# Order of an analysis stage in a wavelet attention and FFN kernel: second level of one chunk ahead of the transposes, and two buffers for the high band

## The chip, the cores and the metric

The kernel runs on one core of one Trainium2 chip. The metric is device time in microseconds; 1209.41 us is the median of three runs of the kernel before. The engines are TensorE (PE: matmuls and transposes), VectorE (DVE), ScalarE (ACT), GpSimd (POOL) and SyncE (SP, which issues most transfers). Each runs its own list of instructions in order; they meet at semaphores only.

## The reference

Two stages follow each other, each with a residual and a layer norm.

```python
# mixer, x is (2, 4096, 512)
for _ in range(2):                       # two levels of analysis
    l = dwconv(low, h_filter)[:, ::2]    # 4 taps a channel, every second sample
    h = dwconv(low, g_filter)[:, ::2]
    highs.append(h); low = l
low = linear_attention(low, 16)          # q = k = elu(h) + 1; kv and z are sums over all positions
for h, L in zip(reversed(highs), reversed(lens)):   # two levels of synthesis
    low = dwconv(repeat(low, 2), h_synth) + dwconv(repeat(h, 2), g_synth)
x = layer_norm(x + layer_norm(x + low) * gamma + beta)
# FFN, int32 weights scaled by 1/127, hidden size 1536
x = layer_norm(x + (silu(x @ wg.T) * (x @ wu.T)) @ wd.T)
```

## The kernel before

The sequence is cut into slices of 1024 positions, four to a batch (`PER_BATCH`), and the 512 channels into four chunks of 128 partitions. The FFN runs slice by slice on TensorE, from eight iterations of `body`; analysis, attention and norms of later slices lie beside it. Attention needs sums over a whole batch, so the four slices of batch 0, and slice 4 (the first of batch 1), are analysed before the first iteration. This is **the opening**, `NPRO` = 5 slices, and the change lies in it.

In a slice a of the opening chunks 0 and 1 are filtered by ScalarE (first tap: `pro_l1`, `pro_band_firsts`) and VectorE (the other taps: `pro_low1_taps`, `pro_band_taps`). Chunks 2 and 3 are filtered by TensorE with matmuls against diagonal matrices (`conv1` for level 1, `conv2` for level 2), and ScalarE copies the results out of PSUM (`pro_out1_copy`, `pro_out2_copy`). A level-1 result is `l1` or `l1_odd`, a level-2 low band `l2` or `l2_odd`, by the parity of a; the level-2 high band is `h2_in` for slice 0, else `h2`, and SyncE stores it to `h2_scratch` (`pro_h2_store`, semaphore `st_h2`).

A slice behind, the keys are made: `pro_keys` on ScalarE, `pro_keys_sum` on VectorE, then `pro_turn` on TensorE (16 transposes to PSUM), `pro_turn_copy` on ScalarE, `pro_kv` on TensorE (64 small matmuls) and `pro_kv_add` on VectorE. SyncE stores the keys (`pro_q_store`). `pro_diags` on ScalarE makes 28 more diagonal matrices of 128 x 128 from the identity, 10 a slice in slices 1 to 3; the close of the opening uses them.

In slice 4 the denominators follow (`pro_heads`, `pro_dens`, and `dens` on VectorE with a reciprocal); SyncE's `dens` spreads them over partitions in four transfers into `att` (semaphores `ld_att`). GpSimd waits for the last of them (chunk 1) and then issues the twelve weight pieces (`load_weights`, a transfer with a cast from int32 to float16 into `w16`, 1536 columns each) and, behind them in its list, the small steps of the first norms (`CLOSE_POOL`). The tables `CLOSE_PE`, `CLOSE_ACT` and `CLOSE_DVE` give the order of the close: attention products, synthesis of slice 0, norms, and the first gate matmuls.

ScalarE writes a buffer again only when its store has landed:

```python
if a > 1:
    act.wait_ge(turned, NC * (a - 1))
    act.wait_ge(st_h2, 16 * a)
    act.wait_ge(pro_halo, 1)
```

`hold` is such a wait followed by a no-operation, so that a transfer is issued behind it. Input loads of slice a+1 (`load_pro`) are issued in slice a, each when its buffer has been read: chunk 3 behind `conv1(a, 3)`, chunks 0 and 1 behind the level-1 taps, chunk 2 behind `conv1(a, 2)`.

## Time and profile before

| | us |
|---|---|
| median of 3 runs (lowest to highest) | 1209.41 (1209.27 to 1209.95) |
| profiled execution, its own time | 1209.61 |
| profiled execution, its span | 1207.8 |
| TensorE busy | 1173.7 |
| VectorE busy | 973.1 |
| ScalarE busy | 672.6 |
| GpSimd busy | 303.1 |
| first gate matmul starts at | 120.81 |

The span is what the profile covers of the execution; the rest of its own time lies around it. TensorE's busy time includes the idle-looking latency of its last matmul in a row, so two of its rows can overlap by some tenths of a microsecond: a group's length is read from the start of one row to the start of the next. The clock that was granted to TensorE is 1.00 at 2.4 GHz and 0.50 at 1.2 GHz. In a row of the timeline the first number is the start, the second the time from there to the end of the last instruction in it, and the brackets at its end give the idle time before it and what ended that.

### The profile page before, as it was taken

The numbers are of one execution on the slowest core, as the hardware profiler recorded it, in microseconds if no ns is written. First come the engines' busy times: TensorE is split into PE (matmuls) and PEld (weight loads), VectorE is DVE, ScalarE is ACT, GpSimd is POOL, SyncE is SP. The second block draws the span as 40 slices with busy tenths as digits, with TensorE's granted clock in tenths as the row PEclk, the third lists the DMA queues.
The fourth block names the chain that finished last, engine by engine and source line by source line (L and its number), as shares of the span: only waits on it lengthen the run. The fifth ranks groups of instructions, "written<-read, shape, count | busy, mean of one in ns | idle before, by whom it ended". The sixth has DMA issues, their size and how long they took to land.

```text
span 1207.8 us, 19489 instructions
## 1 busy us (share of the span) xinstructions
PE 1173.7 (97%) x6456; PEld 604.4 (50%) x6456; DVE 973.1 (81%) x1951; ACT 672.6 (56%) x1403; POOL 303.1 (25%) x730
## 2 busy tenths in 40 slices
PE   6888999999999999999999999999999999999997
PEld 5567644445445544445445444444445444454443
DVE  7797999998999989997997779867997689845331
ACT  6954744677346854576346644666346644565342
POOL 0014322152314313152213412142304313131101
PEclk9998999999999999999999999999999999999999
DMA  7886520222212310222102310211111310110000
GB/s 263 271 201 142 184 61 19 106 97 89 71 44 79 128 40 18 98 83 74 36 27 97 98 35 18 105 62 53 35 58 64 106 35 11 42 55 1 3 34 35
DMA packets 52301, 92.96 MB, mean 77 GB/s; under 512 B 9072, under 2 KB 28784, under 8 KB 51312
## 3 DMA queue, kind: packets, MB, share of 16 engines
q1 hardware_dynamic: 50480, 87.10, 21.9%
q0 software_dynamic: 1728, 4.72, 2.2%
q8 instruction: 46, 0.75, 0.3%
q14 instruction: 47, 0.39, 0.1%
HBM read 67.09 MB, written 25.19 MB: 76 GB/s over the span
## 4 chain that ended last, share of the span: by engine, by line
PE 81%; DVE 6%; ACT 5%; issue 4%; POOL 3%; DMA 1%; SPq 0%; POOLq 0%; ACTq 0%; DVEq 0%
PE ps_up L679 12%; PE ps_up L680 12%; PE ps_gate L679 12%; PE ps_gate L680 12%; PE ps_down L698 12%; PE ps_down L697 12%; PE ps_x L622 2%; PE ps_y L640 2%; DVE l L1286 1%; PE ps_x L601 1%; POOL rs L1216 1%; PE ps_down L864 1%; DVE h L1286 1%; ACT x_hi L1136 1%; DVE hid L1286 1%
## 5 line engine op out<-in xcount | busy, mean ns | idle before, releaser
L697 PE MATMUL ps_down<-w,hid 128*128 128x512 f16 x768 | 291.4, 379 | 1.2 <-DVE hid L1672 1.0
L698 PE MATMUL ps_down<-w,hid 128*128 128x512 f16 x768 | 291.3, 379 | 0.0
L679 PE MATMUL ps_up<-x_hi,w 128*128 128x512 f16 x760 | 288.4, 379 | 0.9 <-DVE h_f L1685 0.9
L679 PE MATMUL ps_gate<-x_hi,w 128*128 128x512 f16 x760 | 288.4, 379 | 0.5 <-ACT h_f L1160 0.5
L680 PE MATMUL ps_gate<-x_lo,w 128*128 128x512 f16 x760 | 288.3, 379 | 0.0
L680 PE MATMUL ps_up<-x_lo,w 128*128 128x512 f16 x760 | 288.2, 379 | 0.0
L1160 ACT ACTIVATE h_f<-ps_gate 128x512 f32<-128x512 f32 x192 | 113.9, 593 | 205.6 <-PE ps_gate L680 204.6
L1685 DVE SCALAR_TENSOR_TENSOR h_f<-ps_up,h_f 128x512 f32<-128x512 f32 x192 | 130.9, 685 | 110.1 <-PE ps_up L680 97.7
L1152 ACT ACTIVATE hid<-h_f 128x512 f16<-128x512 f32 x192 | 119.7, 623 | 42.0 <-DVE h_f L1685 42.0
L1672 DVE TENSOR_TENSOR hid<-h_f,hid 128x512 f16<-128x512 f32 x192 | 130.9, 682 | 1.9 <-ACT hid L1152 1.0
L679 PEld LDWEIGHTS ps_up<-x_hi,w 128*128 128x128 f16 x760 | 74.2, 98 | 91.5 <-DVE h_f L1685 1.8
L680 PEld LDWEIGHTS ps_up<-x_lo,w 128*128 128x128 f16 x760 | 74.3, 98 | 89.4
L697 PEld LDWEIGHTS ps_down<-w,hid 128*128 128x128 f16 x768 | 75.0, 98 | 85.2 <-issue 1.5
L698 PEld LDWEIGHTS ps_down<-w,hid 128*128 128x128 f16 x768 | 75.1, 98 | 84.2
L679 PEld LDWEIGHTS ps_gate<-x_hi,w 128*128 128x128 f16 x760 | 74.2, 98 | 83.0 <-ACT h_f L1160 2.0
L680 PEld LDWEIGHTS ps_gate<-x_lo,w 128*128 128x128 f16 x760 | 74.3, 98 | 82.7
L1213 POOL TENSOR_SCALAR rs<-rs 128x1 f32<-128x1 f32 x128 | 46.4, 363 | 216.5 <-ACT x_hi L1136 142.6
L1286 DVE SCALAR_TENSOR_TENSOR s_chan<-low,coef,s_chan 128x512 f32<-128x512 f32 x140 | 98.8, 747 | 1.0
L1216 POOL TENSOR_TENSOR rs<-rs,minus_half 128x1 f32<-128x1 f32 x128 | 95.8, 749 | 10.7
L1699 DVE SCALAR_TENSOR_TENSOR x<-ps_down,x 128x512 f32<-128x512 f32 x64 | 44.1, 689 | 55.5 <-PE ps_down L698 54.9
L966 ACT ACTIVATE x<-x,rs 128x512 f32<-128x512 f32 x64 | 51.8, 809 | 64.3 <-POOL rs L1218 64.2
L1192 POOL TENSOR_TENSOR rs<-rs,minus_part 128x1 f32<-128x1 f32 x64 | 18.8, 294 | 212.6 <-ACT x L945 212.1
(260 smaller groups left out, 1688.0 us busy)
## 6 DMA issues: line engine op xcount, KB each, us to landing
xt<-x_tok SPq DMA_DIRECT2D x64, 256.0 KB, 2.7
out<-x SPq DMA_DIRECT2D x64, 256.0 KB, 2.0
xb<-x_chan SPq DMA_DIRECT2D x7, 2060.0 KB, 7.7
xa<-x_chan SPq DMA_DIRECT2D x20, 515.0 KB, 5.0
w<-weights POOLq DMA_DIRECT2D x12, 384.0 KB, 9.9
att<-den SPq DMA_DIRECT2D x32, 129.5 KB, 2.7
xa<-x_phase SPq DMA_DIRECT2D x8, 515.0 KB, 6.4
q_in<-q_scratch SPq DMA_DIRECT2D x7, 518.0 KB, 4.5
```

What stands on the lines that cost most here:

```text
L679: pe.matmul(ps_gu[k % 2][g][:, :], w, x1_hi[:, b, c, :], start=(c == 0), stop=False)
L680: mm = pe.matmul(ps_gu[k % 2][g][:, :], w, x1_lo[:, b, c, :], start=False, stop=(c == NC - 1))
L697: pe.matmul(ps_d[t % 2][:, :], h_hi[:, k, t * P:(t + 1) * P], w, start=(k == 0), stop=False)
L698: mm = pe.matmul(ps_d[t % 2][:, :], h_lo[:, k, t * P:(t + 1) * P], w, start=False, stop=(k == NH - 1))
L966: nc.scalar.activation(x1[:, t, :], x1[:, t, :], ACT.Identity, bias=rs2[:, t, 5:6], scale=rs2[:, t, 4:5]).then_inc(x1_ready, 1)
L1152: nc.scalar.activation(h_hi[:, k, :], h_f[:, k % RING, :], ACT.Copy).then_inc(hi_done, 1)
L1160: nc.scalar.activation(h_f[:, k % RING, :], ps_gu[k % 2][0][:, :], ACT.Silu, scale=WSCALE / X1_SCALE).then_inc(silu_done, 1)
L1213: nc.gpsimd.tensor_scalar(rs[:, 3:4], rs[:, 2:3], shrink / C, eps * shrink, ALU.mult, ALU.add).then_inc(var, 1)
L1216: nc.gpsimd.tensor_tensor(rs[:, 4:5], rs[:, 3:4], minus_half[:, :], ALU.pow).then_inc(rstd, 1)
L1286: return V.scalar_tensor_tensor(out=acc, in0=src, scalar=coef[:, c, n:n + 1], in1=acc if add is None else add, op0=ALU.mult, op1=ALU.add)
L1672: V.tensor_tensor(h_lo[:, k, :], h_f[:, k % RING, :], h_hi[:, k, :], ALU.subtract).then_inc(lo_done, 1)
L1685: V.scalar_tensor_tensor(out=h_f[:, k % RING, :], in0=ps_gu[k % 2][1][:, :], scalar=WSCALE * H_SCALE / X1_SCALE, in1=h_f[:, k % RING, :], ...
```

## The change

In five places:

- **TensorE.** `conv2(a, 3)` moves ahead of the transposes of slice a-1, directly behind the two level-1 groups. `pro_kv` comes behind `conv2(a, 2)`; in slice 4 it stays ahead of it.
- **ScalarE.** The 28 diagonals are spread by `DIAGS`: 4 before everything, 5 behind the band firsts of slice 0, 3 each behind the turn copies of slices 1, 2 and 3, and in slice 4 five ahead of the band firsts and five behind the turn copies. The first taps of slice a+1 (`pro_l1`) move ahead of the second pair of level-2 copies.
- **High band.** The odd slices use a new buffer `h2_odd`, which lies in the last two pieces' room of `w16`; its stores count on `st_h2_odd`. A write waits for the store of two slices back (`h2_free`), and GpSimd waits for both odd stores before it issues the tenth and later weight pieces (index 10).
- **SyncE.** The loads of chunks 2 and 3 of `xb` move from slices 1 and 2 to slice 4, behind the high-band store of slice 3; the four token loads follow; then the key store of slice 3 and the denominators' broadcast; the four input loads of slice 5 come behind the broadcast, and the zero pads behind them.
- **VectorE.** The four `xbeta` adds move ahead of the wait for `pro_out2`.

```diff
+DIAGS = ((0, 4), (4, 5), (9, 3), (12, 3), (15, 3), (23, 5), (18, 5))
@@
+        h2_odd = w16[:, PIECES * PW - 2 * NC * M2:PIECES * PW].bitcast(F32).rearrange("p (c n) -> p c n", c=NC)
@@
+        h2_pro = (h2_in[:, :, 1:1 + M2], h2_odd, h2[:, :, :], h2_odd, h2[:, :, :])
+
         def h2_of(a, c):
-            return h2_in[:, c, 1:1 + M2] if a == 0 else h2[:, c, :]
+            return h2_pro[a][:, c, :]
+
+        def st_h2_of(a):
+            return st_h2 if a % 2 == 0 else st_h2_odd
+
+        def h2_free(eng, a):
+            if a > 2:
+                hold(eng, st_h2_of(a), 16 if a == 3 else 32)
@@ load_bands
-                hold(sp, st_h2, 16 * PER_BATCH * (batch + 1))
+                hold(sp, st_h2_odd, 32)
+                hold(sp, st_h2, 16 * PER_BATCH * (batch + 1) - 32)
@@ SyncE, the opening
                 if a > 0:
                     pro_h2_store(a - 1)
+                    if a == PER_BATCH:
+                        for c in (2, 3):
+                            sp.dma_start(xb[:, c, :], x_chan[:, 0, c, :]).then_inc(ld_xb0, 16)
+                        for t in range(4):
+                            load_xt(0, t)
+                    if a == PER_BATCH:
+                        pro_q_store(a - 1)
+                        dens(0, 0, 0)
                     hold(sp, pro_conv1, 2 * a + 1)
                     load_pro(a + 1, 3)
                     hold(sp, pro_low1, 6 * (a + 1))
                     load_pro(a + 1, 0)
                     load_pro(a + 1, 1)
-                    pro_q_store(a - 1)
+                    if a < PER_BATCH:
+                        pro_q_store(a - 1)
                     hold(sp, pro_conv1, 2 * a + 2)
                     load_pro(a + 1, 2)
-                if a in (1, 2):
-                    sp.dma_start(xb[:, a + 1, :], x_chan[:, 0, a + 1, :]).then_inc(ld_xb0, 16)
-                if a == PER_BATCH:
-                    for t in range(4):
-                        load_xt(0, t)
-
-            dens(0, 0, 0)
@@ TensorE
                 conv1(a, 3)
                 conv1(a, 2)
+                conv2(a, 3)
                 if a > 0:
                     for c in range(NC):
                         pro_turn(a - 1, c)
                 if a == PER_BATCH:
                     pro_dens()
                     pro_kv(a - 1)
-                conv2(a, 3)
+                conv2(a, 2)
                 if 0 < a < PER_BATCH:
                     pro_kv(a - 1)
-                conv2(a, 2)
@@ ScalarE, pro_band_firsts and pro_out2_copy
-                    act.wait_ge(st_h2, 16 * a)
+                    h2_free(act, a)
@@ ScalarE, the opening
+                    pro_diags(*DIAGS[0])
...
+                if a == PER_BATCH:
+                    pro_diags(*DIAGS[a + 2])
                 pro_band_firsts(a, 0)
                 pro_band_firsts(a, 1)
+                if a == 0:
+                    act.wait_ge(coef_ready, 6)
+                    pro_diags(*DIAGS[1])
...
-                if a == 1:
-                    act.wait_ge(coef_ready, 6)
-                if 1 <= a <= 3:
-                    pro_diags(10 * (a - 1), 10)
+                if a > 0:
+                    pro_diags(*DIAGS[a + 1])
                 pro_out2_copy(a, 3)
-                pro_out2_copy(a, 2)
                 if a < PER_BATCH:
                     pro_l1(a + 1, 0)
                     pro_l1(a + 1, 1)
+                pro_out2_copy(a, 2)
                 pro_keys(a, 0)
@@ GpSimd, load_weights
+                    if n == PIECES - 2:
+                        nc.gpsimd.wait_ge(st_h2_odd, 32)
@@ VectorE, behind the last slice
+            for t in range(DSUB):
+                xbeta(0, 0, t)
             dve.wait_ge(pro_out2, 2 * NPRO)
```

TensorE's list in slice 1, from the last level-1 group to the last level-2 group, in the kernel before (`kvt_mem` holds the diagonals, `hid` holds `l1_odd` as well as the turned keys; `ps_gate1` and `ps_up1` serve level 1 and the transposes):

```order
L747 MATMUL ps_up0<-xa,kvt_mem 64x257 x4
L782 MATMUL ps_x<-ident,q_in 128x128 x2
L782 MATMUL ps_x<-ident,l2 128x128 x2
L782 MATMUL ps_y<-ident,q_in 128x128 x2
L782 MATMUL ps_y<-ident,l2 128x128 x2
L782 MATMUL ps_gate1<-ident,q_in 128x128 x2
L782 MATMUL ps_gate1<-ident,l2 128x128 x2
L782 MATMUL ps_up1<-ident,q_in 128x128 x2
L782 MATMUL ps_up1<-ident,l2 128x128 x2
L763 MATMUL ps_down0<-hid,kvt_mem 64x256 x8
L572 MATMUL ps_x<-hid 32x32 x32
L763 MATMUL ps_down1<-hid,kvt_mem 64x256 x8
```

And in the kernel after:

```order
L761 MATMUL ps_up0<-xa,kvt_mem 64x257 x4
L777 MATMUL ps_down0<-hid,kvt_mem 64x256 x8
L796 MATMUL ps_x<-ident,q_in 128x128 x2
L796 MATMUL ps_x<-ident,l2 128x128 x2
L796 MATMUL ps_y<-ident,q_in 128x128 x2
L796 MATMUL ps_y<-ident,l2 128x128 x2
L796 MATMUL ps_gate1<-ident,q_in 128x128 x2
L796 MATMUL ps_gate1<-ident,l2 128x128 x2
L796 MATMUL ps_up1<-ident,q_in 128x128 x2
L796 MATMUL ps_up1<-ident,l2 128x128 x2
L777 MATMUL ps_down1<-hid,kvt_mem 64x256 x8
L586 MATMUL ps_x<-hid 32x32 x32
```

The group of eight matmuls to `ps_down0` (level 2 of chunk 3; order counts a matmul of four passes once) has gone ahead of the transposes, and the small products behind the group to `ps_down1`.

ScalarE's list of the same slice, from the diagonals to the keys, before:

```order
L983 ACTIVATE kvt_mem<-ident,coef 128x128 x8
L983 ACTIVATE h_f<-ident,coef 128x128 x2
L980 ACTIVATE hid<-ps_down0 128x256
L980 ACTIVATE h2<-ps_down0 128x256
L980 ACTIVATE hid<-ps_down1 128x256
L980 ACTIVATE h2<-ps_down1 128x256
L983 ACTIVATE l1<-xa,coef 128x514 x2
L1045 ACTIVATE keys<-hid 128x512
L1047 ACTIVATE keys<-keys 128x512
L1045 ACTIVATE keys<-hid 128x512
L1047 ACTIVATE keys<-keys 128x512
```

After:

```order
L997 ACTIVATE h_f<-ident,coef 128x128 x3
L994 ACTIVATE hid<-ps_down0 128x256
L994 ACTIVATE w16<-ps_down0 128x256
L997 ACTIVATE l1<-xa,coef 128x514 x2
L994 ACTIVATE hid<-ps_down1 128x256
L994 ACTIVATE w16<-ps_down1 128x256
L1059 ACTIVATE keys<-hid 128x512
L1061 ACTIVATE keys<-keys 128x512
L1059 ACTIVATE keys<-hid 128x512
L1061 ACTIVATE keys<-keys 128x512
```

Three diagonals stand where ten stood, the copies to `h2` go to `w16`, and the first taps of slice 2 (`l1<-xa,coef`) stand between the two pairs of copies.

SyncE's list at the end of the opening, before:

```order
L415 DMA xa<-x_phase 128x1030
L486 DMA h2_scratch<-h2 128x4x256
L408 DMA xa<-x_chan 128x1030 x3
L491 DMA q_scratch<-keys 128x4x256
L408 DMA xa<-x_chan 128x1030
L450 DMA xt<-x_tok 128x512 x4
L470 DMA att<-den 128x1x259 x4
L528 DMA q_scratch<-zeros 1024x1x1
L528 DMA q_scratch<-zeros 1024x1x2
```

After:

```order
L426 DMA xa<-x_phase 128x1030
L497 DMA h2_scratch<-w16 128x4x256
L523 DMA xb<-x_chan 128x1030 x2
L462 DMA xt<-x_tok 128x512 x4
L502 DMA q_scratch<-keys 128x4x256
L482 DMA att<-den 128x1x259 x4
L419 DMA xa<-x_chan 128x1030 x4
L542 DMA q_scratch<-zeros 1024x1x1
L542 DMA q_scratch<-zeros 1024x1x2
```

The broadcast (`att<-den`) has two loads of `xb` and the token loads ahead of it and no load of `xa`; the four of `xa` come behind it.

## Rows read from the trace of the kernel before

**Rows 1.** The page: busy time of the fullest engine, share of the span, instructions.

```profile
PE 1173.7 (97%) x6456; PEld 604.4 (50%) x6456; DVE 973.1 (81%) x1951; ACT 672.6 (56%) x1403; POOL 303.1 (25%) x730
```

**Rows 2.** Busy times by stretch, length first; then clock, transfers' busy share, GB/s.

```profile
core 0: us, PE busy (x) PEld busy (x) DVE busy (x) ACT busy (x) POOL busy (x), PEclk, DMA share, GB/s
...
44.60:55.60 11.00, 8.71 (x121) 6.31 (x120) 10.69 (x28) 10.42 (x27) 0.00 (x0) 0.84 0.86 280
...
105.90:111.20 5.30, 5.29 (x13) 4.22 (x14) 4.46 (x11) 2.22 (x5) 4.15 (x8) 0.50 0.86 214
...
120.70:1207.80 1087.10, 1077.53 (x5559) 529.25 (x5557) 877.70 (x1691) 595.89 (x1207) 284.12 (x679) 1.00 0.18 61
```

**Rows 3.** Timeline of VectorE, slices 2 to 4 (start, length, engine, line, operation).

```profile
31.47 4.08 DVE L1286 SCALAR_TENSOR_TENSOR l<-xa,coef,l 128x514 f32<-128x514 f32 x6 [1.73 <-ACT l L983]
...
44.59 4.07 DVE L1286 SCALAR_TENSOR_TENSOR hid<-xa,coef,hid 128x513 f32<-128x513 f32 x6 [2.40 <-ACT hid L983]
...
50.20 0.48 DVE L1286 SCALAR_TENSOR_TENSOR hid<-hid,coef 128x256 f32<-128x256 f32 x1
...
55.27 0.29 DVE L1542 TENSOR_TENSOR kv_sum<-ps_x,kv_sum 128x128 f32<-128x128 f32 x1 [0.23 <-PE ps_x L572]
58.49 4.08 DVE L1286 SCALAR_TENSOR_TENSOR l<-xa,coef,l 128x513 f32<-128x513 f32 x6 [2.93 <-ACT l L983]
```

**Rows 4.** Timeline of ScalarE in slice 3: first taps, band firsts, diagonals, level-2 copies.

```profile
43.76 1.46 ACT L983 ACTIVATE hid<-xa,coef 128x513 f32<-128x513 f32 x2
...
48.65 0.53 ACT L983 ACTIVATE hid<-hid,coef 128x256 f32<-128x256 f32 x1 [0.52 <-DMA h_scratch<-h]
...
52.79 1.30 ACT L983 ACTIVATE h_f<-ident,coef 128x128 f32<-128x128 f32 x4
...
55.13 0.39 ACT L980 ACTIVATE hid<-ps_down 128x256 f32<-128x256 f32 x1
```

**Rows 5.** Timeline of TensorE: level 1 of chunk 2 (slice 2), transposes, level 2.

```profile
32.57 1.13 PE L747 MATMUL ps_gate<-xa,kvt_mem 128*64 128x257 f32 x8 [0.76 <-DMA xa<-x_phase]
...
49.06 0.44 PE L782 MATMUL ps_x<-ident,keys 128*128 128x128 f32 x2 [2.29 <-DVE keys L1526]
...
51.78 2.75 PE L763 MATMUL ps_down<-hid,kvt_mem 128*64 128x256 f32 x16
...
55.16 1.95 PE L763 MATMUL ps_down<-hid,kvt_mem 128*64 128x256 f32 x16
```

**Rows 6.** Transfers from 0 to 110 us: KB each, median us to landing.

```profile
xa<-x_phase SPq DMA_DIRECT2D x8, 515.0 KB, 6.4
...
h_scratch<-h SPq DMA_DIRECT2D x3, 512.0 KB, 4.5
```

**Rows 7.** The page, transfers of the whole kernel: the denominators' broadcast.

```profile
att<-den SPq DMA_DIRECT2D x32, 129.5 KB, 2.7
```

**Rows 8.** The chain of waits, in order of time: start, length.

```profile
71.84 5.83 DMA att<-den
```

**Rows 9.** The weight transfers: shortest, median and longest time to landing.

```profile
DMA to landing us min/median/max: 4.5/9.9/15.4
```

**Rows 10.** Timeline of GpSimd and of ScalarE's first norm step, 78 to 101 us.

```profile
78.29 3.95 POOL L1187 DMA_DIRECT2D w<-weights  x7 [36.09 <-DMA att<-den]
...
97.22 0.19 ACT L945 ACTIVATION_READ_ACCUMULATOR x<-ps_x 128x1 f32 x1
97.44 2.66 POOL L1187 DMA_DIRECT2D w<-weights  x5 [15.20 <-issue]
...
100.07 0.25 POOL L1192 TENSOR_TENSOR rs<-rs,minus_part 128x1 f32<-128x1 f32 x1
```

**Rows 11.** Busy times by stretch, as in rows 2, beside the weight transfers.

```profile
80.00:82.00 2.00, 2.00 (x20) 2.00 (x19) 2.00 (x6) 0.21 (x2) 2.00 (x5) 1.00 0.90 51
...
84.00:86.00 2.00, 2.00 (x11) 1.74 (x11) 2.00 (x7) 0.47 (x2) 0.00 (x0) 1.00 1.08 211
```

**Rows 12.** Timeline of VectorE: the first attention product.

```profile
77.17 0.43 DVE L1556 TENSOR_TENSOR att<-ps_x,att 128x259 f32<-128x259 f32 x1
```

More of the change, by code:

```diff
@@ L1660, in _ @@
                        "norm2b": lambda t: norm2_scale(0, t), "norm3": lambda t: norm3(0, 0, t)}
-            for t in range(DSUB):
-                xbeta(0, 0, t)
             for name, n in CLOSE_DVE:
```

11 lines of the change are left out of this document (5 added, 6 removed).

## Prediction

> **What bounds the kernel now.** I read the page first, for which engine is full: TensorE, 97% of the span [rows 1]. The busy times by stretch say where that holds [rows 2]. From 120.70 us on TensorE is busy for 1077.53 of 1087.10 us, so nothing that the change touches there can move the time. Before that lies the opening, in which four stages follow each other: five slices of analysis (to about 72.6 us), the close of the attention, and the first norms. Whatever makes the first gate matmul start earlier shortens the kernel by as much. The profiled execution took 1209.61 us for its span of 1207.8, 0.2 above the median of 1209.41; a shift in the span is taken off the median.
>
> The timeline of VectorE shows what the slices wait for [rows 3]. Its low-band taps of slices 2, 3 and 4 start at 31.47, 44.59 and 58.49 us, each behind an idle time of 1.73, 2.40 and 2.93 us, ended by ScalarE. So the distance between two starts is over 13 us, and VectorE's own work in it is 5.61 us (taps and key sums, 44.59 to 50.20), 4.84 us (second-level taps, to 55.27 less 0.23 idle) and 0.28 us: 10.7 us. ScalarE, which ends those waits, runs the first taps last, behind eight to ten diagonals and four copies [rows 4]. TensorE in turn idles 2.29 us before the transposes, and its clock reads 0.84 over that slice, which means some of it at 1.2 GHz [rows 2, 5].
>
> Behind the slices, the chain of waits goes: denominators, their broadcast (landing at 77.67, 5.83 us after the issue), GpSimd's weight DMAs, GpSimd's first norm at 100.07 [rows 8, 10]. GpSimd starts seven weight pieces at 78.29, stands still for 15.20 us, issues the other five for 2.66 us, and only then does the norm that ScalarE had ready at 97.41 [rows 10]. The 15.4 us of the slowest piece [rows 9] show that the eighth is issued about when the seventh (issued at 81.7) has landed. All behind it, to the first gate matmul, is in a row with that norm, so what counts is when the weight train ends.
>
> **Slices.** The first taps of slice a+1 now stand ahead of the second pair of level-2 copies, and the diagonals are spread: 4 at the start, where ScalarE waits for the input, 5 in slice 0, then 3, 3, 3 and 10 in slice 4. One diagonal is 0.29 us (eight from 52.79 to 55.13 [rows 4]). In slice 1 that takes 7 diagonals and 2 copies (0.53 us) out of the way: 2.6 us against a wait of 1.73, so VectorE starts slice 2 without one, at 29.7. The five in slice 0 delay TensorE's second-level group of chunk 2 by 1.5 us, but the keys behind it wait for VectorE's taps anyway; cost nothing, and 1.5 if that cover were gone.
>
> From there ScalarE needs per slice: first taps, keys and level-1 copy 4.37 us (43.76 to 48.65 less 0.52 idle), band firsts, copy and turns 4.14 us (48.65 to 52.79), 3 diagonals 0.88, level-2 copies 1.1: 10.5 us, below VectorE's 10.7. The 0.52 us wait for the store of the high band goes, since the store two slices back has landed (4.5 us for such a store [rows 6]; it now has over 15). TensorE is the third: four groups of 16 matmuls at 1.95 us, transposes about 1.8, products 0.7: 10.3 us [rows 5]. Level 2 of chunk 3 ahead of the transposes fills its 2.29 us of idle time. This order has a price: the transposes now come behind a group that wants the load of chunk 2. In slice 2 that load lands at 32.57 [rows 5], 1.1 us after the old start but 2.8 us after the new one. Two groups (3.7 us) and the first transposes (0.4) behind it end at 36.9, where ScalarE, 6.25 us into the slice, would be at 35.95: 0.9 us late, of which about 0.5 is left after the slack between 10.5 and 10.7. In the next slices everything, the issue of the load too, has moved with the slice, so there I take 0 to 0.3. Starts: 29.7, 40.8, 51.4, against 58.49: **7.1 us earlier**. Bounds: 8.0 (a pace of 10.4) down to 4.1 (rival 1). The clock at 1.2 GHz in slice 3 stood behind TensorE's idle stretch; with under 1 us of idle time per slice I expect full clock.
>
> Moving bytes is not far from a bound either. A slice stores 1.0 and loads 2.1 MB, 3.1 MB in 10.8 us: 287 GB/s, where the rows show 280 at a busy share of 0.86, so 326 when full [rows 2]. The two loads of chunks 2 and 3 for the close no longer lie in slices 1 and 2, which is what makes room.
>
> Writing the high band into the weights' room, and the taps on it, is not in the trace. Same partitions, same widths as the old buffer; I take zero, with plus or minus 0.1 us per slice.
>
> **Slice 4.** Five diagonals (1.5 us) ahead of the band firsts: ScalarE is ready about 55.4, the firsts run 56.9 to 58.6, VectorE could start them at 57.65 and waits 0.3. The transposes come after level 2 of chunk 3, and the denominators need turn copies 0 and 1 (60.1), so their product ends at 60.9, 0.5 us behind VectorE's chunk 0. Together 0.7 us given back: denominators ready **6.35 us earlier**. The other five diagonals lie where ScalarE waits for TensorE.
>
> **SyncE's queue and the broadcast.** Before, 4.1 MB were issued from the last high-band store to the broadcast, the last of it just ahead, and the broadcast landed 5.83 us after its issue [rows 8]. Now it is 3.1 MB (store 0.5, two loads 1.0, tokens 1.0, keys 0.5), issued from 52.6 to 57.5 and moved at 326 GB/s by about 63, when the broadcast is issued. Over the kernel such a broadcast lands in 2.7 us [rows 7]. Between 2.7 and 5.83 I take 3.0, nearest to the first since the queue is then empty: **2.8 us earlier** on top, bounds 0 and 3.1. The loads for the close land by 62.5 and are wanted at 63.6; the tokens land before their adds, which ends a 0.9 us wait of VectorE's.
>
> **The weight train.** The four loads of slice 5 (2.06 MB, 6.3 us at 326 GB/s) and the four zero-pad DMAs no longer precede the weights but run beside them. Before, the train took from 78.29 to 97.1, 18.8 us; seven pieces of 393 KB at 211 GB/s are 13.0 of it [rows 9 to 11]. Now the loads are issued from 66.4 on and the first piece at 69.2. About 3 us pass before weight bytes move, in which 4 us of the loads are done; some 1.9 us of loads and 1.2 us more of pads stay in front or beside: **3.1 us later**. Bounds: 0 and 6.3. The wait for the odd stores before the tenth piece costs nothing: behind it are two pieces and all the norms on GpSimd, but the store landed near 57. The extra hold on SyncE before each later band load has half an iteration's slack.
>
> **Sum.** 6.35 + 2.8 - 3.1 = 6.0 us for GpSimd's first norm: 94.1 instead of 100.07. The other path, VectorE's first attention product (at 77.17 [rows 12]), moves by 6.15 + 0.9 = 7.0 us, so ScalarE's 97.41 becomes 90.4: still earlier than GpSimd, and the train decides. Behind it the same row of waits follows, 1.2 GHz stretch included (clock 0.50 from 105.90 to 111.20 [rows 2]). 1209.41 - 6.0 = **1203.4 us**.
>
> A rule speaks to the last term. The trace shows 51 GB/s at a busy share of 0.90 from 80 to 82 us, when pads and weights overlap, so pads do take room [rows 11]. The Trainium skill, DMA: Bandwidth & Descriptors, Queues, rings and completion order, has each DMA engine take turns between queues packet by packet; by it the tiny pads would cost the weights next to nothing. That makes the fourth case below.
>
> **Rivals.**
> 1. *The load of chunk 2 sets the pace.* If it lands 1 us later in each slice (6.4 us is the median from issue to landing [rows 6]; it now stands before level 2, the transposes and their copies), the pace is 11.9: 3 us less, 1206.4. For it: TensorE has no slack left. Against: fewer bytes in the queue.
> 2. *The broadcast lands as late as before*, 5.8 us after the issue: 2.8 us less, 1206.2. Against: the queue runs empty by my count.
> 3. *The change does not do what it says*: another wait takes the whole of each stall (keys waiting for their store, say), and only the exchange in the queue is left, 2.8 - 3.1: 1209.7.
> 4. *The train is no longer than before* (18.8 us), because loads and pads use only the time in which its first piece is being prepared: GpSimd is free 6.35 + 2.8 = 9.1 us earlier, and VectorE's path decides with 7.0: 1202.4.
> 5. *Slower: TensorE at 1.2 GHz through the slices.* A group of 16 took 2.75 instead of 1.95 us in slice 3 [rows 5]: 4 x 2.75 + 2.7 + 0.7 = 14.4 us per slice against 13.1 now, 3 x 1.3 = 3.9 us later, and 0.3 for the queue: 1213.6. It decides from a pace of 13.0 on. Against: TensorE idles less than before.
>
> **How the numbers follow.** Forecast 0.52, rival 1 0.17, rival 2 0.08, rival 3 0.06, rival 4 0.12, rival 5 0.05. The range, 1201.0 to 1208.0, reaches from rival 4 with 1.4 us for the 1.2 GHz stretch in the norms to rivals 1 and 2 with their spread; outside lie 3, 5 and tails, about 0.2. A measurement of this kernel tells 0.2% (2.4 us) from no change. Faster: the first two, fourth and forecast, less the tail of rivals 1 and 2, 0.83; within 0.2%: 0.11; slower: 0.06.
>
> **What would show it.** Right: no idle time of VectorE over 0.5 us before the taps of slices 2 to 4, which start near 29.7, 40.8 and 51.4; clock 1.00 in them; broadcast landing near 68.5, first weight piece near 69.2, GpSimd's first norm near 94, first gate matmul near 114.7. Wrong if the load of chunk 2 keeps TensorE waiting over 2 us per slice, or if GpSimd's pause exceeds 19 us.

## The result and the profile after

The changed kernel ran in 1201.28 us (median of 4 runs, 1199.3 to 1201.86) beside 1209.68 for the kernel before: a ratio of 0.9926, interval 0.9912 to 0.9940. That is 8.4 us faster where 6.0 were forecast. Taken off the 1209.41 of the forecast by its ratio it is 1200.5, a little below the range on record (1201.0 to 1208.0); 1201.28 as it stands lies just inside it. In two later series, each on a chip of its own, it had 1205.17 us (6 runs, 1202.72 to 1207.17; ratio 0.9972, 0.9960 to 0.9984) and 1202.73 (5 runs, 1201.39 to 1204.34; 0.9951, 0.9938 to 0.9965). All 15 runs together have a median of 1202.73, about 6 below before. That this is the forecast of 6.0 is luck, as its terms will show. So two things need a cause: where the terms of the forecast went in the profiled execution, and why one kernel spreads over 8 us.

The profiled execution took 1201.81 us, its span 1200.0, against 1207.8. The page, to be held against [rows 1]:

```profile
PE 1170.5 (98%) x6456; PEld 601.5 (50%) x6456; DVE 972.8 (81%) x1951; ACT 673.0 (56%) x1403; POOL 303.4 (25%) x730
```

The busy times by stretch (columns as in [rows 2]): two stretches of slice 0, the last group of the close (at 0.50 from 105.90 before), and all from the first gate matmul on.

```profile
16.00:18.00 2.00, 1.37 (x10) 0.84 (x12) 2.00 (x6) 2.00 (x7) 0.00 (x0) 0.77 0.56 196
18.00:20.00 2.00, 2.00 (x12) 1.21 (x10) 2.00 (x5) 0.48 (x2) 0.00 (x0) 0.50 0.00 0
100.90:105.30 4.40, 4.40 (x21) 3.82 (x22) 3.82 (x10) 2.22 (x5) 3.25 (x8) 1.00 1.08 237
113.00:1200.00 1087.00, 1077.47 (x5558) 529.76 (x5556) 877.20 (x1691) 595.98 (x1207) 284.44 (x679) 1.00 0.19 61
```

From the first gate matmul (113.06 us, before 120.81) to the end it is the same 1087 us: all of the gain lies ahead of it. VectorE's low-band taps, the answer to [rows 3], start slices 2, 3 and 4 at 30.41, 42.27 and 54.39; the rest of each group waits once more, for ScalarE, whose own wait there was for the load of a chunk:

```profile
30.41 0.76 DVE L1306 SCALAR_TENSOR_TENSOR l<-xa,coef,l 128x514 f32<-128x514 f32 x1
31.44 3.41 DVE L1306 SCALAR_TENSOR_TENSOR l<-xa,coef,l 128x514 f32<-128x514 f32 x5 [0.27 <-ACT l L997]
42.27 0.75 DVE L1306 SCALAR_TENSOR_TENSOR hid<-xa,coef,hid 128x513 f32<-128x513 f32 x1 [0.37 <-ACT hid L997]
43.56 3.40 DVE L1306 SCALAR_TENSOR_TENSOR hid<-xa,coef,hid 128x513 f32<-128x513 f32 x5 [0.54 <-ACT hid L997]
54.39 4.07 DVE L1306 SCALAR_TENSOR_TENSOR l<-xa,coef,l 128x513 f32<-128x513 f32 x6
```

TensorE, to be read against [rows 5]: in slice 0 it now waits 2.15 us for the copy behind the five diagonals, and the group of 16 behind that gap takes 3.28 us; in slices 2 to 4 it waits for the load of chunk 2.

```profile
16.63 3.28 PE L777 MATMUL ps_down<-l,kvt_mem 128*64 128x256 f32 x16 [2.15 <-ACT l L994]
33.31 1.13 PE L761 MATMUL ps_gate<-xa,kvt_mem 128*64 128x257 f32 x8 [1.25 <-DMA xa<-x_phase]
45.61 0.22 PE L757 MATMUL ps_gate<-zeros,kvt_mem 128*64 128x1 f32 x1 [1.84 <-DMA xa<-x_phase]
56.58 0.22 PE L754 MATMUL ps_gate<-zeros,kvt_mem 128*64 128x1 f32 x1 [0.32 <-DMA xa<-x_phase]
```

Behind the slices, the broadcast from SyncE's queue (second fence: the landing of its last transfer by the chain of waits, 3.04 us, where [rows 8] has 5.83), then GpSimd's weights and first norm, against 78.29, 15.20 and 100.07 in [rows 10]:

```profile
66.49 3.26 SPq L482 DMA_DIRECT2D att<-den  x4
```

```profile
69.15 3.04 DMA att<-den
```

```profile
72.81 3.95 POOL L1207 DMA_DIRECT2D w<-weights  x7 [31.36 <-DMA att<-den]
92.44 2.66 POOL L1207 DMA_DIRECT2D w<-weights  x5 [15.68 <-issue]
95.06 0.25 POOL L1212 TENSOR_TENSOR rs<-rs,minus_part 128x1 f32<-128x1 f32 x1
```

The rest of the 7.75 us is in TensorE's last group of the close, 20 matmuls. Before, it ran from 105.91 to 113.05, 7.1 us, most of it at half clock; now it takes 4.4. First twelve matmuls before, then after:

```profile
105.91 2.90 PE L864 MATMUL ps_down<-h,h_f 128*128 128x256 f32 x6 [3.12 <-ACT hid L980]
108.59 2.77 PE L864 MATMUL ps_down<-hid,h_f 128*128 128x256 f32 x6
```

```profile
100.90 1.53 PE L878 MATMUL ps_down<-h,h_f 128*128 128x256 f32 x6 [3.01 <-ACT hid L994]
102.27 1.46 PE L878 MATMUL ps_down<-hid,h_f 128*128 128x256 f32 x6
```

So 5.0 us come with GpSimd's norm, and 2.7 from a clock that did not fall. From that norm to the start of the group it is 5.84 us in both.

### The profile page after: what moved, and what is told of

It is laid out like the page before. It is cut to its first block, busy times and chain, and to the rows that moved or that the text cites. A ratio compares the mean times of both kernels' runs of the same rounds, so it can differ in the third digit from the quotient of the medians.

```text
span 1200.0 us, 19493 instructions
## 1 busy us (share of the span) xinstructions
PE 1170.5 (98%) x6456; PEld 601.5 (50%) x6456; DVE 972.8 (81%) x1951; ACT 673.0 (56%) x1403; POOL 303.4 (25%) x730
## 4 chain that ended last, share of the span: by engine, by line
PE 81%; DVE 6%; ACT 4%; issue 4%; POOL 3%; DMA 2%; SPq 0%; POOLq 0%; DVEq 0%; ACTq 0%
PE ps_up L693 13%; PE ps_up L694 13%; PE ps_gate L693 12%; PE ps_gate L694 12%; PE ps_down L711 12%; PE ps_down L712 12%; PE ps_x L636 2%; PE ps_y L654 2%; DVE l L1306 2%; PE ps_x L615 1%; POOL rs L1236 1%; DVE h L1306 1%; PE ps_down L878 1%; DMA xa<-x_phase 1%; ACT x_hi L1154 1%
## 5 line engine op out<-in xcount | busy, mean ns | idle before, releaser
L1236 POOL TENSOR_TENSOR rs<-rs,minus_half 128x1 f32<-128x1 f32 x128 | 95.9, 749 | 10.7
## 6 DMA issues: line engine op xcount, KB each, us to landing
w<-weights POOLq DMA_DIRECT2D x12, 384.0 KB, 11.1
```

Of the source, the lines that this page charges most:

```text
L1236: nc.gpsimd.tensor_tensor(rs[:, 4:5], rs[:, 3:4], minus_half[:, :], ALU.pow).then_inc(rstd, 1)
```

## The experiments

Four questions: what the clock does ahead of that group, what each half of the change brings, what the five diagonals of slice 0 cost, and what holds the pace of the slices. A last part tries a version that beats both kernels. Each series had the kernel before on the same chip, with medians 1208.94 (e1 to e4), 1209.10 (e5 to e8), 1208.69 (e9 to e12), 1208.74 (e13 to e16).

**The clock ahead of the last group.** The filler covers TensorE's gap there with work that nobody reads.

```diff
+            def fill(n):
+                pe.wait_ge(pro_low_ready, 8)
+                for _ in range(n):
+                    pe.matmul(ps_d[0][:, 0:P], ident[:, :], ident[:, :], start=True, stop=True)
...
-("norm1", 2), ("s", (2, 1)), ("norm1", 3),
+("norm1", 2), ("fill", 11), ("s", (2, 1)), ("norm1", 3),
```

> The kernel before, with 11 small matmuls (identity by identity, into a bank that is overwritten next) put into TensorE's idle time of 3.1 us ahead of the synthesis group at 105.91 us. Theory: the 2.8 us that the changed kernel gains behind GpSimd's first norm are TensorE's clock, which stayed at 2.4 GHz in it and read 0.50 from 105.9 to 111.2 us in the kernel before. Then this kernel keeps 1.00 there, its synthesis group of 20 matmuls takes 4.4 us instead of 7.3, and it is 2.5 to 3.0 us faster. Rival: the gain comes from the new order of loads and adds (earlier tokens, no pads in the way); then filling the gap is worth 0, within 0.3 us.

The kernel before with the filler: 1206.90 us (11 runs), ratio 0.9984 (0.9975 to 0.9993). In the trace the group, from 105.39 on, takes 1.53, 1.46, 1.03 and 1.03 us for its pieces, 4.4 in all instead of 7.1, and the first gate matmul comes at 117.54, 3.3 earlier, of which 0.55 is an earlier start of the weights (77.74). The trace gives the 2.7 us that the theory wanted (2.5 to 3.0); the medians give 2.0, less than it wanted, and far from the rival's 0.3.

> The changed kernel with eleven extra matmuls (identity by identity, into a bank that nobody reads any more) between the third transposes of the first norm and the last group of the close, in the only long gap of TensorE ahead of that group. Theory (2.8 us of the result come from the clock, which no longer falls ahead of this group): the changed kernel already has the full clock there in most executions, so the filler brings next to nothing: 0 to 0.7 us faster, first gate matmul between 112.5 and 113.1 us. Rival (the matmuls fill, as such, changes something else that saves 2 us, as a shorter wait behind the group): it would save about 2 us here too, first gate matmul near 111.

Measured: 1202.43 us, ratio 0.9949 (0.9936 to 0.9961), first gate matmul at 112.91, as the theory had it (112.5 to 113.1), so the rival's 111 is out. It is 0.15 earlier than in the profile of after, which had the clock whole there. Against that profile the filler gives nothing, so it is worth only what the clock takes. (This series had no changed kernel without it on the same chip.)

> The changed kernel as it is, so that the runs beside it have it on the same chip. Its first four runs gave a median of 1201.28 us. Theory (time before the first gate matmul is given away whenever TensorE's clock falls, and where it falls differs from execution to execution): the runs spread over 3 us or more, with the mean granted clock of the slower ones below that of the faster, median 1201 to 1203.5. Rival (the kernel has one time): the spread stays under 1.5 us.

The changed kernel, unchanged: 1205.17 us, ratio 0.9972, above the 1201 to 1203.5 that was expected, with the spread that was expected (4.5 us). Of its six runs the fastest, 1202.72, has a mean granted clock of 0.998, and the two at 0.997 took 1204.11 and 1206.05 and the three at 0.995 took 1204.87 to 1207.17. The profile is of the fastest. Even in it the same group fell to the lower clock, and its first twelve matmuls, behind a gap of 2.39 us, took 4.35 us where the profile of after has 2.66 (100.90 to 103.56):

```profile
99.99 2.10 PE L878 MATMUL ps_down<-h,h_f 128*128 128x256 f32 x6 [2.39 <-ACT hid L994]
101.88 2.62 PE L878 MATMUL ps_down<-hid,h_f 128*128 128x256 f32 x6
```

> The changed kernel once more, beside e14 to e16 on the same chip. Theory (it has two kinds of execution, with the clock whole and with the clock down ahead of the last group of the close): runs between 1199.5 and 1207, the lower ones at a mean clock of 0.998 or more, median 1201 to 1205. Rival (the difference between 1201.28 and 1205.17 is the chip's, not the execution's): all runs within 1.5 us of each other.

> The changed kernel with the eleven matmuls in the gap ahead of the last group of the close, as e5. Theory: the median is 1 to 3 us below that of e13, the range at its upper end smaller, last group 4.4 us in the trace. Rival (the filler is worth nothing, the kernel has simply a spread): median and spread as e13's, within 0.7 us.

On one chip: 1202.73 us for the changed kernel (1201.39 to 1204.34), 1201.02 with the filler (1200.43 to 1201.81), ratios 0.9951 and 0.9939. The medians are 1.7 us apart, the spread is 2.95 against 1.4 us. The intervals of the ratios (0.9938 to 0.9965 and 0.9926 to 0.9953) overlap, so five runs of each make the filler's gain likely; the trace is what shows it, with a group of 4.4 us (e14) against 6.1 (e13). In e13's trace the gap ahead of the group is 3.01 us, to the digit that of the first profile, and this time the clock fell. The timeline, and the stretch by its busy times, with a granted clock of 0.61 (third number from the right):

```profile
99.00 2.03 PE L878 MATMUL ps_down<-h,h_f 128*128 128x256 f32 x6 [3.01 <-ACT hid L994]
100.83 2.69 PE L878 MATMUL ps_down<-hid,h_f 128*128 128x256 f32 x6
```

```profile
99.00:103.40 4.40, 4.40 (x13) 3.54 (x14) 3.83 (x10) 2.23 (x5) 3.25 (x8) 0.61 1.08 237
```

Over all profiled executions without a filler (before, after, e2, e3, e4, e8, e9, e13) the gap is 2.0 to 3.1 us and the clock fell in seven of eight; the exception is the profile of after. In the ten with a filler it is 0.7 us at most and the clock fell in none. The length of the gap alone does not decide, though. In e8 TensorE stood 3.70 us in slice 2, longer than anywhere above, and the clock stayed whole behind it (1.00, third number from the right in the stretch):

```profile
35.36 1.13 PE L761 MATMUL ps_gate<-xa,kvt_mem 128*64 128x257 f32 x8 [3.70 <-DMA xa<-x_phase]
```

```profile
36.00:38.00 2.00, 2.00 (x20) 1.23 (x17) 1.97 (x8) 1.03 (x4) 0.42 (x2) 1.00 1.06 268
```

The kernel before has both in one execution: 2.31 us ahead of the transposes of slice 1, clock whole, and 2.29 us ahead of those of slice 3 [rows 5], clock down.

The rival, that the difference between 1201.28 and 1205.17 is the chip's, is not excluded. Its mark, all runs of e13 within 1.5 us of each other, is missed (2.95). Nor is the theory of two kinds of execution shown: e13's profiled one, with the clock down in the last group, took 1201.94 us, and the first profile, with the clock whole there, 1201.81, since e13's slice 4 started 3 us earlier.

**The two halves of the change.**

Kernel e2 is the one before with SyncE's loop as changed, e3 the changed one with SyncE's loop as before:

```diff
+                    if a == PER_BATCH:
+                        for c in (2, 3):
+                            sp.dma_start(xb[:, c, :], x_chan[:, 0, c, :]).then_inc(ld_xb0, 16)
+                        for t in range(4):
+                            load_xt(0, t)
+                    if a == PER_BATCH:
+                        pro_q_store(a - 1)
+                        dens(0, 0, 0)
```

> The kernel before with SyncE's new order alone (loads for the close in slice 4, broadcast ahead of the loads of slice 5). Theory: the slices start as before (58.5 us for the last), since ScalarE sets their pace there; the broadcast lands 2.4 us sooner after its issue and the weight train is 0.5 us longer, so GpSimd's first norm moves by 1.5 to 2.5 us, and with the smaller gap the clock may stay up: 2 to 5 us faster. Rival (the prediction's price for the train, 3.1 us): about 0, within 0.5 us.

> The kernel after with SyncE's old order: the two loads for the close back in slices 1 and 2, the loads of slice 5 ahead of the broadcast. Theory that the queue of loads sets the slices' pace: two more loads of 0.5 MB in slices 1 and 2 make the starts of slices 3 and 4 0.5 to 2 us later than 42.3 and 54.4, the broadcast lands 2.4 us later, and the kernel is 3 to 6 us slower than the kernel after. Rival that ScalarE's and TensorE's order sets the pace: same starts, 2 us slower.

e2: 1205.93 us, ratio 0.9972 (0.9963 to 0.9982). The slices start as before (31.16, 44.14, 58.03), the weights at 74.59 instead of 78.29, the first norm at 97.13, the first gate matmul at 116.81. e3: 1205.93 us, 0.9977 (0.9967 to 0.9987): slice 4 at 55.53, weights at 75.36, first norm at 97.33, first gate matmul at 117.01. In e2 the slices did not move and the first norm came 2.9 us earlier, more than the 1.5 to 2.5 of the theory; the rival, no change, is out. In e3 slice 3 did not come later than in the profile of after (41.86 against 42.27), slice 4 came 1.1 us later, and the time is 3 to 6 us above the changed kernel's 1201.28 as expected, but on another chip.

Alone the queue brings 4.0 us at the first gate matmul and the rest of the change 3.8; together, 7.75. That the sum fits is luck. At GpSimd's first norm the two bring 2.9 and 2.7, 5.7 in all, where the profile of after has 5.0; behind it they bring 1.06 each, since the clock fell only in part of the last group, where after has 2.7. The clock fell in other places in each of the three (in slice 0 it held in e3 and fell in after), so whether the halves add up is not shown. Each alone is worth about half.

**The diagonals of slice 0.**

```diff
-                if a == 0:
-                    act.wait_ge(coef_ready, 6)
-                    pro_diags(*DIAGS[1])
                 pro_out1_copy(a, 2)
 ...
                 pro_out2_copy(a, 2)
+                if a == 0:
+                    act.wait_ge(coef_ready, 6)
+                    pro_diags(*DIAGS[1])
                 pro_keys(a, 0)
```

> The kernel after with the five diagonals of slice 0 behind the last level-2 copy instead of ahead of the level-1 copy of chunk 2. Theory: there they let TensorE idle 2.15 us, the clock fell to 1.2 GHz, the first store was issued at 20.7 instead of 19.3 us and the next load of chunk 3 at 22.2 instead of 19.8, and all loads behind them in the queue were late. Without that: clock 1.00 from 16 to 22 us, slice 2 starts by 29.8 instead of 30.4 and slice 4 by 53.5 instead of 54.4, kernel 0.8 to 2 us faster. Rival (the prediction: cover hides it): 0, within 0.3 us.

> The changed kernel with the five slice-0 diagonals behind the level-2 copies, as e4, and the filler as well. In e4 the first norm came 1.8 us earlier and the group behind it gave 1.7 us back at a clock of 1.2 GHz. Theory: with the filler the group takes 4.4 us instead of about 6, first gate matmul near 111.3, 1.5 to 1.9 us faster than the changed kernel. Rival (the gain of e4 was lost to something later in the chain than the clock, as the other path through VectorE): first gate matmul stays near 112.9.

> As e14, and eight more matmuls, identity by identity, between the two second-level groups of slice 0, where TensorE waits 2.15 us for the diagonals. Theory (the five diagonals cost their delay of 1.5 us, and behind it the clock: the group behind the gap took 3.28 instead of 1.95 us at a granted clock of 0.50): the group takes 1.95 us, the store of slice 0's high band and the loads behind it are issued 1.0 to 1.3 us earlier, slice 4 starts 0.4 to 1.3 us earlier than 54.39. Rival (the clock falls there whatever TensorE does, or the loads do not hang on it): group over 2.7 us, or slice 4 within 0.3 us of 54.4.

e4: 1202.65 us, ratio 0.9947 (0.9934 to 0.9960), not the 0.8 to 2 us below 1201.28 that was expected. Slice 4 starts at 52.47, 1.9 us earlier than in the profile of after, the first norm comes at 93.25, 1.8 earlier, and the first gate matmul at 112.92, 0.14 earlier: the last group fell to the lower clock and took the gain. With the filler (e6) the group takes its 4.4 us and the first gate matmul comes at 111.47, 1.6 us earlier than in after; the median, 1201.81 us (ratio 0.9945), doesn't show it, in a spread of 1200.16 to 1205.03.

e15 leaves the diagonals where they are and covers only the gap that they make: 1201.41 us, 0.9937 (0.9924 to 0.9951), slice 4 at 52.20, first gate matmul at 110.95, the earliest of all kernels that give the reference's output. Its slice 0 and that of e13, where nothing covers the gap:

```profile
15.09 2.05 PE L896 MATMUL ps_x<-ident 128*128 128x128 f32 x16
17.07 1.95 PE L777 MATMUL ps_down<-l,kvt_mem 128*64 128x256 f32 x16
```

```profile
16.68 1.95 PE L777 MATMUL ps_down<-l,kvt_mem 128*64 128x256 f32 x16 [1.82 <-ACT l L994]
```

The other profiles help here. Up to slice 4 their lists are those of after, but for the filler in slice 0 of e15 and the place of the diagonals in the row of e4. The gap in slice 0, the group of 16 behind it, and the starts of slices 2, 3 and 4:

| | gap | group | slice 2 | slice 3 | slice 4 |
|---|---|---|---|---|---|
| after | 2.15 | 3.28 | 30.41 | 42.27 | 54.39 |
| e5 | 2.15 | 3.62 | 30.89 | 42.22 | 54.03 |
| e11 | 2.05 | 2.76 | 30.98 | 42.33 | 54.48 |
| e9 | 1.39 | 1.95 | 29.37 | 41.03 | 53.06 |
| e14 | 1.25 | 1.95 | 29.21 | 40.90 | 52.94 |
| e13 | 1.82 | 1.95 | 29.28 | 40.21 | 51.43 |
| e15 (gap filled) | none | 1.95 | 29.52 | 41.06 | 52.20 |
| e4, e6, e12, e16 (diagonals later) | 0.42 to 0.64 | 1.95 | 29.30 to 29.64 | 40.66 to 40.95 | 52.47 to 53.18 |
| forecast | | | 29.7 | 40.8 | 51.4 |

So the diagonals' delay by itself costs nothing that shows: with the clock whole, slice 2 starts at 29.2 to 29.5 with them in place and at 29.3 to 29.6 without. Where the clock fell behind the gap it starts 0.9 to 1.8 us later than with the diagonals and the clock whole, and slice 4 is still 0.8 us or more later. In the profile of after, with 3.28 us for the group, the store of slice 0's high band is issued at 20.69 instead of 19.41 (e13), the load behind it at 22.17 instead of 20.55. The 1.5 us that e15's text gives the delay was wrong; moving the diagonals helps because the gap shrinks (0.60 us in e6). e15 went the way of its theory, but not by its sizes: the store came at 19.80, 0.9 us earlier instead of 1.0 to 1.3, and slice 4 2.2 us earlier instead of 0.4 to 1.3. The slices behind slice 2 spread by more than the clock explains: from slice 2 to slice 4 the seven rows need 22.2 to 24.0 us.

**The pace of the slices.**

e7, SyncE's order:

```diff
                     load_pro(a + 1, 1)
-                    if a < PER_BATCH:
-                        pro_q_store(a - 1)
                     hold(sp, pro_conv1, 2 * a + 2)
                     load_pro(a + 1, 2)
+                    if a < PER_BATCH:
+                        pro_q_store(a - 1)
```

> The changed kernel with the filler and with the store of the keys (0.5 MB) behind the load of chunk 2 in SyncE's queue instead of ahead of it, in slices 1 to 3. Theory (TensorE's waits of 1.25, 1.84 and 0.32 us for that load in slices 2 to 4 hold the pace): they shrink by up to 1.6 us (0.5 MB at 326 GB/s), slice 4 starts 1 to 2.5 us earlier than the 54.39 of the changed kernel, and the first gate matmul 1 to 2 us earlier. Rival (the pace is held by the loads of chunks 0 and 1, for which ScalarE waits, or by the late start in slice 0): slice 4 starts within 0.5 us of 54.4, no change of the time.

The theory falls: TensorE no longer waits for chunk 2 in any slice, yet slices 2 and 3 start at 30.99 and 41.88 (its second chunk 43.09), where e5, with the filler alone and the same half clock in slice 0, has 30.89 and 42.22 (43.15). The wait has only moved, to ScalarE's keys, which want the late store landed; behind it TensorE stood 2.54 us, and its clock fell (3.57 us for the group), so slice 4 starts at 56.84. Time 1202.99 us, ratio 0.9945.

```profile
45.40 0.63 ACT L1065 ACTIVATE keys<-l 128x512 f32<-128x512 f32 x1 [1.81 <-DMA q_scratch<-keys]
48.47 3.57 PE L777 MATMUL ps_down<-hid,kvt_mem 128*64 128x256 f32 x16 [2.54 <-ACT hid L1000]
```

e8, TensorE's order:

```diff
                 conv1(a, 2)
-                conv2(a, 3)
                 if a > 0:
                     for c in range(NC):
                         pro_turn(a - 1, c)
...
+                conv2(a, 3)
                 conv2(a, 2)
```

> The changed kernel with TensorE's order of before: level 2 of chunk 3 behind the transposes, all else as changed. Theory (this reorder is what takes TensorE's 2.3 us of idle time away, the price being the wait for chunk 2's load): slice 4 starts 1.0 to 3.0 us later than 54.39, the time is 1 to 3 us longer than the changed kernel's. Rival (with the wait for the load the reorder gains nothing net, the gain is ScalarE's): slice 4 within 0.5 us of 54.4, same time.

With TensorE's old order slices 3 and 4 start at 43.87 and 55.10 (second chunk 56.36). Against the 54.39 of after that is 0.7 us later, between the theory (1.0 to 3.0) and the rival (0.5). But here the clock of slice 0 held, and against the profiles in which it held too (e9, e13, e14) the second chunk is 2.1 to 3.7 us later. In this profile one wait for chunk 2 is 3.70 us, so the wait that I feared from the new order is there without it. The time, 1202.98 us over a spread of 8 (1200.99 to 1209.26; ratio 0.9956), decides nothing; one trace speaks for the reorder.

e10, with the keys' store cut alike:

```diff
-                sp.dma_start(h2_dram[:, 0, :, a * M2 + 1:(a + 1) * M2 + 1], h2_pro[a])
+                sp.dma_start(h2_dram[:, 0, :, a * M2 + 1:a * M2 + 65], h2_pro[a][:, :, 0:64])
```

> The kernel of e6 with the stores of keys and high band in slices 0 to 3 cut from 256 columns to 64, so 0.26 MB a slice instead of 1.05; what is left out is written behind the opening with other values, so the output of the first block is not the reference's. Theory (the 3.1 MB that a slice moves hold its pace near 11.7 us, through whichever load is wanted first): with 2.35 MB the waits for loads go and slices 2, 3 and 4 start 10.6 to 10.9 us apart, slice 4 near 51.2 instead of 53.18. Rival (the loads are late because they are issued late in the slice, and their time from issue to landing does not come from the bytes beside them): landings stay 5.5 to 7.5 us, slice 4 within 0.5 us of 53.2.

Slices 2, 3 and 4 start at 29.30, 40.44 and 51.65, 11.14 and 11.21 us apart, where e6 has 11.34 and 12.23. First the two stretches of e10, then those of e6; the second column is the length, the fourth VectorE's busy time:

```profile
29.30:40.44 11.14, 10.29 (x148) 6.61 (x146) 10.80 (x30) 10.59 (x25) 0.76 (x4) 1.00 0.76 225
40.44:51.65 11.21, 10.87 (x156) 7.71 (x153) 10.79 (x29) 10.55 (x26) 0.00 (x0) 1.00 0.75 215
```

```profile
29.61:40.95 11.34, 10.58 (x152) 7.24 (x150) 10.69 (x29) 10.33 (x25) 0.86 (x4) 1.00 0.84 264
40.95:53.18 12.23, 10.13 (x150) 7.53 (x148) 10.93 (x29) 10.92 (x26) 0.00 (x0) 1.00 0.89 289
```

VectorE's own work is 10.8 us, as the prediction had it (10.7); what stands above it is waiting, 0.3 and 0.4 us a slice with small stores, 0.65 and 1.3 with the full ones. Three more profiles have e6's lists up to slice 4 (e4, e12, e16): with e6 they need 11.06 to 11.39 us from slice 2 to slice 3, where e10 has 11.14, and 11.78 to 12.27 from there to slice 4, where e10 has 11.21. So a quarter fewer bytes buy nothing in the first stretch and 0.6 to 1.1 us in the second; slice 4 is 0.8 to 1.5 us earlier, at 51.65. The rival's 53.2 within 0.5 is out, and the theory's 10.6 to 10.9 us a slice is not reached. How the bytes do it is only half seen: the loads' time from issue to landing hardly changes (channel loads 5.8 us, 5.6 in e6; phase loads 5.9 and 6.2), as the rival said, while the stores of the keys land in 6.0 instead of 7.4 us, and ScalarE's waits for them, 0.55 and 0.35 us in e6, are gone. The first gate matmul comes at 109.49, 2.0 us earlier than in e6. The time, 1200.83 us, shows less of it: from there to the end this kernel takes 1088.4 us instead of 1087, perhaps for the columns that it writes behind the opening.

**GpSimd's norms, and a version beyond both.**

```diff
-            load_weights(0, PIECES)
+            load_weights(0, 7)
+            behind = {("norm1", 1): 7, ("norm2", 1): 8, ("norm2", 2): 9, ("norm1q", 3): 10, ("norm2", 3): 11}
             for name, t in CLOSE_POOL:
                 steps[name](0, 0, t)
+                if (name, t) in behind:
+                    load_weights(behind[name, t], 1)
```

> The changed kernel with the filler, and with GpSimd's last five weight pieces put one by one between its norm instructions instead of ahead of them all. Theory (GpSimd stands still until the seventh piece has landed, so the row of norms waits for the weight train, and without that it would wait only for ScalarE, which has x ready at 93.27 us against 95.06 in GpSimd): first norm at 93.3, first gate matmul 1.0 to 1.8 us earlier (111.3 to 112.1), time 1.0 to 1.8 us shorter than the changed kernel's. Rival (the issues between the norms, 0.53 us each, or the late pieces give it back): first gate matmul at 112.9 or later.

> Three of these together on the changed kernel: slice-0 diagonals later (e6), filler (e5), norms between the weight pieces (e11). Theory: 1.6 us from the diagonals and 1.0 to 1.8 from the norms add up, since the path through VectorE and ScalarE moves with the slices: first gate matmul at 109.7 to 110.5, 1198.5 to 1200 us. Rival (the path through VectorE's attention products does not move with the diagonals, as it is held by the broadcast): no more than either alone, first gate matmul near 111.4.

> The kernel of e12 (diagonals of slice 0 later, filler, norms between the weight pieces) again, on another chip beside the changed kernel. Theory: 2.5 to 4.5 us below e13 and 1.0 to 2.5 below e14, ratio to the kernel before 0.992 to 0.9935. Rival (its 1200.04 us was luck of the executions): within 1 us of e14.

In e11 GpSimd's first norm starts at 93.44, when ScalarE has x ready, but takes 0.97 us instead of 0.25; the next starts at 95.42, against 96.09 in e5, and the first gate matmul at 112.34, 0.6 earlier: less than the 1.0 expected, since half of the gain went into that slow first instruction. Time 1201.65 us, 0.9940 (0.9927 to 0.9954), on the chip where the changed kernel had 1205.17. e12, with the diagonals later: first gate matmul at 111.03, later than the 109.7 to 110.5 of its theory, 1200.04 us, 0.9935 (0.9922 to 0.9949). Against e5 (112.91) the diagonals alone bring 1.4 us there (e6), the norms alone 0.6 and both 1.9, so they nearly add; the theory had both terms too large. e16, the same on another chip: 1200.69 us, 0.9935, beside 1202.73 for the changed kernel and 1201.02 with the filler alone. Its theory, 2.5 to 4.5 us below e13 and 1.0 to 2.5 below e14, fails (2.0 and 0.3), and the rival, within 1 us of e14, holds. Its median is below both kernels', but e14 and e15 are as fast within the noise: most of it is the filler's.

## Why the prediction was wrong

By its own steps, for the profiled executions:

- **What bounds the kernel.** Right: the row of waits, the place of the gain, and that GpSimd's norm decides and not the path through VectorE (x ready at 93.27, norm at 95.06).
- **Slices, 7.1 us earlier.** 4.1 in the profile. Two steps failed. One is that the five diagonals in slice 0 "cost nothing, and 1.5 if that cover were gone". The cover held; what was put at nothing is TensorE's own gap of 2.15 us, in a place where it had had none (granted clock 1.00 from 14 to 20 us before), and the half clock behind it, 0.9 to 1.8 us at slice 2. The other is the pace behind slice 2, next point. e13 has the starts of the forecast (29.28, 40.21 and 51.43 against 29.7, 40.8 and 51.4), but it is the best of the profiles: with the clock as whole, e9 and e14 reach slice 4 at 53.06 and 52.94.
- **"In the next slices [...] I take 0 to 0.3".** The clock was full in slices 2 to 4, as forecast, but TensorE's waits for chunk 2 were 1.25, 1.84 and 0.32 us, where the forecast had a delay of 0.9 us in slice 2 (0.7 by its own terms: 32.57 + 3.7 + 0.4 is 36.7) and 0 to 0.3 behind it. The slices lie 11.86 and 12.12 us apart, where the forecast had 11.1 and 10.6 and rival 1 had 11.9. Its 3 us less is what the slices lost here, though in part for the clock of slice 0 and so by luck. Rival 1 had the load right; e10 shows that the bytes beside it have a part, and e7 that without this wait another one (the keys' for their store) takes its place.
- **Slice 4, 0.7 us given back.** 1.1: VectorE waits 0.79 us for the denominators' product (64.18, before 67.21).
- **Broadcast, 2.8 us earlier.** 2.4. The landing took 3.04 us, the 3.0 of the forecast; the four issues took 0.4 us longer than before.
- **Weight train, 3.1 us longer.** 0.5, from 19.15 to 19.63 (19.15, not 18.8, is what [rows 10] gives: 78.29 to 97.44). This step, "some 1.9 us of loads and 1.2 us more of pads stay in front or beside", failed by 2.6 us. In the first stretch of the train, in which weights hardly moved before (51 GB/s in [rows 11]), 389 GB/s passed (rows below), so most of what the loads needed was free, and the weights kept their rate beside the pads. Rival 4 named this mechanism with 0.12. The other profiles with the new queue give 0.3 to 1.4 us, so not quite free. The wait for the odd stores (ahead of index 10, the eleventh piece) cost nothing, as forecast: the last five issues take 2.66 us in both.
- **"The same row of waits follows, 1.2 GHz stretch included".** The row of waits did (5.84 us from norm to group in both), the stretch did not in the profile of after: 2.7 us, of which the range had allowed 1.4. Without it the profile would stand at 1209.41 - 5.0 = 1204.4 us, well inside the range; with it at 1201.7, near its end, and the 0.6 us from there to the medians' 8.4 is spread of the executions. In e4, e9 and e13 the clock did fall, for part of the group. The forecast took a thing that falls one way or the other for a fixed cost.

The weight train by stretches, around the issue of its first seven pieces (72.81 to 76.76 us) and while pads and weights run side by side (last two numbers: share of the DMA engines, GB/s):

```profile
72.00:76.00 4.00, 2.67 (x15) 1.76 (x14) 3.94 (x17) 3.72 (x11) 3.19 (x6) 1.00 0.99 389
78.00:82.00 4.00, 4.00 (x28) 3.74 (x27) 4.00 (x12) 0.56 (x3) 0.00 (x0) 1.00 1.17 212
82.00:86.00 4.00, 4.00 (x20) 3.48 (x20) 3.91 (x13) 0.00 (x0) 0.00 (x0) 1.00 1.16 210
```

SyncE's queue is held by the last two pad DMAs for 15.51 us from 76.28 on, and the weights beside it move at 210 to 212 GB/s, the 211 of [rows 11] without pads. The turn-taking between queues, packet by packet, of the Trainium skill (DMA: Bandwidth & Descriptors, Queues, rings and completion order) fits this; a kernel without the pads was not tried.

In sum 3.03 + 2.45 - 0.48 = 5.0 us at GpSimd's norm instead of 6.0: 3.3 us less from the slices and 2.6 more from the train nearly cancel, which is luck. With 2.7 us of clock on top it is 7.75 of span. In e13 it is 6.9 at the norm (93.17) and 1.1 in the group. The spread between whole runs is explained for the profiled ones only: in all of them but e10 the time from the first gate matmul to the end is 1086.9 to 1087.3 us, so nearly all they differ in lies ahead of it. For the others there is the mean clock. 0.995 instead of 0.998 over 1204 us is, by my estimate, 3.6 us of lost work, which is about what separates e9's median from the first one. But it does not account for all: one run of e7 took 1203.62 us at 1.000 and one of e6, with the filler, 1204.73 at 0.998. Where the clock fell in the runs without a trace is open, what else slows them too, and so is what makes the same gap of 3.01 us end in one clock or the other.

## What to carry to other kernels

A term that ends in a gap of the bounding engine has two prices, the gap and the clock behind it, and the second may fall in one execution and not in the next: look at the clock of a stretch in more than one profile, give the range both, and cover the gap with work that nobody reads before comparing anything finer. It does not end every spread: e6 and e12 have the filler and spread over 4.9 and 4.2 us. When a transfer is moved in front of another one, ask first when the second one's bytes begin to move; here 2 MB passed ahead of them for 0.3 to 1.4 us. And when two terms of a forecast miss by 3 us each, a total that fits proves neither.

## What the runs showed of the hardware

- Ahead of the last group of the close the clock fell behind gaps of TensorE of 2.0 to 3.1 us in seven of eight executions, and never behind 0.7 us or less in ten. In slice 0 it fell behind gaps of 2.05 and 2.15 us in four (after, e5, e7, e11), while behind 2.15 (e8), 1.82, 1.40, 1.39 and 1.25 us it held. It held also behind 3.70 us in slice 2 of e8 and behind 2.22 us in slice 4 of e15, so more than the length of the gap decides.
- GpSimd's stand ahead of its eighth piece of weights was 15.2 to 15.4 us in the three profiled executions with the old queue (before, e1, e3) and 15.45 to 16.6 us in the twelve with the new one that issue the pieces in one row; in e11, e12 and e16 the eighth piece, issued after 95 us, held nothing up.
- GpSimd's first arithmetic behind a stand of 17 us took 0.95 to 0.97 us when it waited for ScalarE (e11, e12, e16) and 0.24 to 0.34 when it came straight behind weight issues.
